# Two quads of value products per visit, maxima padded to 128 columns, and re-dealt places in a cross-attention and expert kernel

## The reference

```python
q = layernorm(x) @ Wq.T + bq;  k = ctx @ Wk.T + bk;  v = ctx @ Wv.T + bv
qk = einsum('bhqd,bhkd->bhqk', q, k)              # no scale
attn = softmax(qk);  z = einsum('bhqk,bhkd->bhqd', attn, v)
a = layernorm(z + layernorm(x)) * gamma + beta;   x2 = x + a
zf = layernorm(layernorm(x2)) * g + b             # then the router
w = top-2 of softmax(zf @ rW + rb), normalised over the two
out = x2 + sum_e w_e * (gelu(zf @ W1_e + b1_e) @ W2_e + b2_e)
```

## Time and profile before

| | |
|---|---|
| median of 3 runs | 846.84 us (845.5 to 849.79) |
| profiled execution, its own time | 850.93 us |
| its span, first to last instruction | 848.7 us |
| mean granted TensorE clock | 0.943 of 2.4 GHz |

### The profile page before, as it was taken

How to read it: one execution, slowest core, us unless ns; L and a number is a source line. 1 busy time by engine, 2 the same in 40 slices (tenths; PEclk the granted TensorE clock), 3 DMA queues, 4 the chain that set the end, 5 groups by cost and what they waited for, 6 DMA issues and landing times.

```text
span 848.7 us, 26242 instructions
## 1 busy us (share of the span) xinstructions
PE 755.9 (89%) x8056; PEld 586.7 (69%) x8057; DVE 631.7 (74%) x1779; ACT 563.4 (66%) x1469; POOL 535.6 (63%) x609
## 2 busy tenths in 40 slices
PE   3689999999999999999999997565979888999994
PEld 2456667767777777777777675344968787999994
DVE  7488998889899998998998898875446673454441
ACT  3346777888888887888888885533655544666662
POOL 3323667677677676876777775317456555777773
PEclk9989999999999999999999999855989998999998
DMA  6756575768768677677687676621334333443441
GB/s 186 170 122 144 125 159 123 161 148 179 161 150 189 140 172 165 152 170 169 147 183 160 160 169 147 195 59 43 57 55 63 51 46 56 75 63 57 67 62 21
DMA packets 154000, 104.43 MB, mean 123 GB/s; under 512 B 68364, under 2 KB 149560, under 8 KB 153816
## 3 DMA queue, kind: packets, MB, share of 16 engines
q1 hardware_dynamic: 133462, 77.42, 41.8%
q0 software_dynamic: 10944, 14.10, 10.3%
q10 hardware_dynamic: 9538, 12.23, 5.1%
HBM read 36.65 MB, written 17.33 MB: 64 GB/s over the span
## 4 chain that ended last, share of the span: by engine, by line
PE 62%; DMA 11%; DVE 8%; issue 6%; POOL 6%; SPq 4%; ACT 2%; DVEq 1%; ACTq 0%; POOLq 0%
PE s_row L988 9%; PE pj L884 8%; PE pj L853 8%; PE s_row L898 7%; PE s_t L917 7%; PE zt L929 7%; PE pj L999 4%; PE zt L999 4%; PE pj L871 3%; SPq L653 2%; DMA stack_x<-in_x 2%; DMA out_x<-index_space,idx_s 2%; DMA zscr<-zn 2%; DVE negmax L1360 2%; DMA stack_x<-k_part 2%
## 5 line engine op out<-in xcount | busy, mean ns | idle before, releaser
L1360 DVE TENSOR_REDUCE negmax<-s_row 100x1 f32<-100x361 f32 x512 | 251.5, 524 | 24.8 <-PE s_row L898 18.9
L1183 ACT ACTIVATE p_t<-s_t 128x400 f32<-128x400 f32 x384 | 187.9, 499 | 85.8 <-PE s_t L917 77.6
L898 PE MATMUL s_row<-stack_x,q_stack 125*128 125x361 bf16 x512 | 133.2, 322 | 18.7 <-DVE negmax L1360 12.8
L721 POOL DMA_INDIRECT out_x<-index_space,idx_s x57 | 92.2, 1617 | 76.3 <-ACT index_space L1168 34.6
L917 PE MATMUL s_t<-q_stack,stack_x 128*128 128x100 bf16 x1536 | 129.4, 211 | 10.9 <-ACT p_t L1183 8.7
L917 PEld LDWEIGHTS s_t<-q_stack,stack_x 128*128 128x128 bf16 x1536 | 93.5, 99 | 57.3 <-issue 30.9
L988 PE MATMUL s_row<-w_qkv,v_aug 128*128 128x128 f32 x912 | 117.8, 285 | 1.2 <-DVE v_aug L1455 1.2
L988 PEld LDWEIGHTS s_row<-w_qkv,v_aug 128*128 128x128 f32 x912 | 113.0, 202 | 1.8 <-DVE v_aug L1455 1.7
L1365 DVE TENSOR_SCALAR p_t<-p_t 128x1200 f32<-128x1200 f32 x128 | 100.0, 781 | 12.8 <-ACT p_t L1183 12.7
L884 PE MATMUL pj<-w_qkv,ct 128*128 128x256 f32 x384 | 106.0, 399 | 0.0
L853 PE MATMUL pj<-ct,w_qkv 128*128 128x361 f32 x256 | 96.1, 500 | 10.3 <-DMA bk_s<-in_bk 9.2
(11 more groups left out here) (232 smaller groups left out, 1423.8 us busy)
## 6 DMA issues: line engine op xcount, KB each, us to landing
stack_x<-k_part SPq DMA_DIRECT2D x192, 192.0 KB, 3.6
q_stack<-q_part SPq DMA_DIRECT2D x192, 64.0 KB, 2.0
ct<-in_ctx_t SPq DMA_DIRECT2D x32, 361.0 KB, 4.3
stack_x<-in_w ACTq DMA_DIRECT2D x8, 512.0 KB, 6.7
w_s<-in_w ACTq DMA_DIRECT2D x14, 256.0 KB, 2.9
zscr<-zn SPq DMA_DIRECT2D x32, 100.0 KB
z_in<-zscr SPq DMA_DIRECT2D x32, 100.0 KB
zf_d<-zf_s SPq DMA_DIRECT2D x32, 100.0 KB
```

The lines of the kernel that those rows point to most:

```text
L721: pool.indirect_dma_start(out_rows[0:n], bass.IndirectOffsetOnAxis(idx_s[:, k.slot:k.slot + 1], 0), ys[:, k.slot, :], None, bounds_check=n ...
L898: nc.tensor.matmul(s_row[h % 2][:, 0:KEYS], q_stack[0:MROW, b.slot, h, :], k_stack[0:MROW, b.slot, h, 0:KEYS], start=True, stop=True).then ...
L1183: nc.scalar.activation(p_t[:, quad % 2, kt, :], s_t[g % 2][:, 0:4 * Q], ACT.Exp).then_inc(exp_done, 1)
L1360: v.tensor_reduce(negmax[:, b.slot, h:h + 1], s_row[h % 2][0:Q, 0:KEYS], AXIS.X, ALU.max, negate=True).then_inc(max_done, 1)
```

## The change

Five things are changed.

1. `values` is called for two quads back to back, in slots 0 and 6 of an iteration, in place of one quad in slots 0, 3, 6 and 9. `p_t` gets a third quad, indexed by `ring`.
2. `m_rows` gets 128 columns, of which 80 are zero, and its transpose writes 128 partitions.
3. `v_raw` is gone to make room: the bias writes `v_aug` and the cleaning works in place. The routing words that used its space move to `k_rest`; `ys` of the expert part moves into `p_t`, and the first expert result waits for the last value products.
4. The places of the pipeline's steady part are changed.
5. The places of batch 0 (`START`) are changed.

```diff
+def ring(b, quad):
+    return (b.slot + quad) % 3
...
-        v_raw = sb(es, "v_raw", [128, KT * H, DH])
-        p_t = sb(es, "p_t", [128, 2, KT, 4 * Q])
+        p_t = sb(es, "p_t", [128, 3, KT, 4 * Q])
...
-            m_rows = sb(att, "m_rows", [Q, 3 * H], BF16)
+            m_rows = sb(att, "m_rows", [Q, 128], BF16)
...
-                    nc.tensor.matmul(tr[0:3 * H, 0:Q], m_rows[:], ident_bf[:], start=True, stop=True).then_inc(mt_done, 1)
+                    nc.tensor.matmul(tr[:, 0:Q], m_rows[:], ident_bf[:], start=True, stop=True).then_inc(mt_done, 1)
...
-                    pe.wait_ge(p_ready, G * b.index + quad + 1)
+                    if quad % 2 == 0:
+                        pe.wait_ge(p_ready, G * b.index + quad + 2)
...
-                                                    p_t[0:n, quad % 2, kt, j * Q:j * Q + Q], start=(kt == 0), stop=(kt == KT - 1))
+                                                    p_t[0:n, ring(b, quad), kt, j * Q:j * Q + Q], start=(kt == 0), stop=(kt == KT - 1))
...
-                        if n.valid() and g % KT == 0:
+                        if n.valid() and g in (KT, 3 * KT):
+                            values(n, g // KT - 1)
                             values(n, g // KT)
...
-                        after(act, pv_done, G * b.index + quad - 1)
-                    nc.scalar.activation(p_t[:, quad % 2, kt, :], s_t[g % 2][:, 0:4 * Q], ACT.Exp).then_inc(exp_done, 1)
+                        after(act, pv_done, G * b.index + quad - 2)
+                    nc.scalar.activation(p_t[:, ring(b, quad), kt, :], s_t[g % 2][:, 0:4 * Q], ACT.Exp).then_inc(exp_done, 1)
...
-                    v.scalar_tensor_tensor(v_aug[:, b.slot, :, 0:DH], v_raw[:], 0.0, v_raw[:], ALU.max, ALU.min).then_inc(v_ready, 1)
+                    biased = v_aug[:, b.slot, :, 0:DH]
+                    v.scalar_tensor_tensor(biased, biased, 0.0, biased, ALU.max, ALU.min).then_inc(v_ready, 1)
...
-SP_PLACE = {"zf": 7, "ctx": 3, "q": 14, "k": 14, "zout": 4, "max": 10, "zin": 14}
+SP_PLACE = {"zf": 1, "ctx": 6, "q": 12, "k": 17, "zout": 9, "max": 11, "zin": 12}
...
-START = {"PE": {"k0": 3, "k1": 3}, "ACT": {"k0": 0, "drow": 1, "k1": 1, "dt": 2, "q": 3, "k_mid": 3, "q_mid": 7}, "DVE": {}, "POOL": {"k_rest": 3, "k_low": 11}, "SP": {}}
+START = {"PE": {"k0": 5, "k1": 13}, "ACT": {"k0": 1, "drow": 0, "k1": 3, "dt": 0, "q": 3, "k_mid": 9, "q_mid": 13}, "DVE": {}, "POOL": {"k_rest": 11, "k_low": 17}, "SP": {}}
```

More of the change, by code:

```diff
@@ L479, in build @@
             q_stack = sb(att, "q_stack", [128, 3, H, QPAD], BF16)
-            index_space = sb(att, "index_space", [128, KT * D])
+            index_space = sb(att, "index_space", [128, 4 * NT])
             negmax = sb(att, "negmax", [Q, 3, H])
-            m_rows = sb(att, "m_rows", [Q, 3 * H], BF16)
+            m_rows = sb(att, "m_rows", [Q, 128], BF16)
             m_rest = sb(att, "m_rest", [Q, H])
@@ L541, in build @@
             base = per_expert(drow[:])
-            idx_at = index_space
-            ys, idx0, idx1, slot_c, second = carve(idx_at, (2 * D, NT, NT, NT, NT))
-            ys = ys.rearrange("p (s d) -> p s d", s=2)
+            idx0, idx1, slot_c, second = carve(index_space, (NT, NT, NT, NT))
+            ys = p_t[:].rearrange("p r k n -> p (r k n)")[:, 0:2 * D].rearrange("p (s d) -> p s d", s=2)
             idx_t = [idx0, idx1]
@@ L1287, in _ @@
                 v.memset(q_part[:, :, :, :, Q:QPAD].rearrange("p a s t k -> p (a s t) k"), 0.0).then_inc(pad_written, 1)
+                v.memset(m_rows[:, 3 * H:], 0.0).then_inc(pad_written, 1)
                 dve.wait_ge(rows_written, 2)
@@ L1338, in values_biased @@
                 def values_biased(b, last):
-                    after(dve, v_ready, b.index)
+                    after(dve, pv_done, G * (b.index - 2))
                     if last:
                         dve.wait_ge(v2_done, b.index + 1)
-                        v.tensor_tensor(v_raw[:, 2 * H:3 * H, :].rearrange("p h d -> p (h d)"), pj[0][:, 0:D],
-                                        bv_s[:, :], ALU.add).then_inc(v2_biased, 1)
+                        v.tensor_tensor(v_aug[:, b.slot, 2 * H:3 * H, 0:DH], pj[0][:, 0:D].rearrange("p (h d) -> p h d", d=DH),
+                                        bv_s[:, :].rearrange("p (h d) -> p h d", d=DH), ALU.add).then_inc(v2_biased, 1)
                     else:
                         dve.wait_ge(v01_done, b.index + 1)
-                        bias2 = bv_s[:, :].unsqueeze(1).broadcast_to([128, 2, D])
-                        v.tensor_tensor(v_raw[:, 0:2 * H, :].rearrange("p (t h) d -> p t (h d)", t=2), pj[1][:, :].rearrange("p (t n) -> p t n", t=2),
-                                        bias2, ALU.add).then_inc(v01_biased, 1)
+                        bias2 = bv_s[:, :].rearrange("p (h d) -> p h d", d=DH).unsqueeze(1).broadcast_to([128, 2, H, DH])
+                        v.tensor_tensor(v_aug[:, b.slot, 0:2 * H, 0:DH].rearrange("p (t h) d -> p t h d", t=2),
+                                        pj[1][:, :].rearrange("p (t h d) -> p t h d", t=2, d=DH), bias2, ALU.add).then_inc(v01_biased, 1)
                 def values_cleaned(b):
-                    after(dve, pv_done, G * (b.index - 2))
                     dve.wait_ge(v2_biased, b.index + 1)
                     dve.wait_ge(v01_biased, b.index + 1)
-                    v.scalar_tensor_tensor(v_aug[:, b.slot, :, 0:DH], v_raw[:], 0.0, v_raw[:], ALU.max, ALU.min).then_inc(v_ready, 1)
+                    biased = v_aug[:, b.slot, :, 0:DH]
+                    v.scalar_tensor_tensor(biased, biased, 0.0, biased, ALU.max, ALU.min).then_inc(v_ready, 1)
                 def row_max(b, h):
@@ L1364, in guard @@
                     dve.wait_ge(exp_done, NG * b.index + KT * quad + KT)
-                    v.tensor_scalar(p_t[:, quad % 2], p_t[:, quad % 2], 0.0, None, ALU.max).then_inc(p_ready, 1)
+                    v.tensor_scalar(p_t[:, ring(b, quad)], p_t[:, ring(b, quad)], 0.0, None, ALU.max).then_inc(p_ready, 1)
                 heads = tr[0:Q, :].rearrange("q (h w) -> q h w", w=32)
@@ L1462, in result @@
                     after(dve, scattered[k.slot], 16 * k.pair)
+                    if k.known and k.index == 0:
+                        dve.wait_ge(pv_done, G * B)
                     v.tensor_scalar(idx_s[:, k.slot:k.slot + 1], idx_t[1][:, bass.ds(k.index, 1)], 0.0, None, ALU.add).then_inc(idx_s_ready, 1)
```

11 lines of the change are left out of this document (6 added, 5 removed).

## The result

The changed kernel takes 858.64 us (857.64 to 860.58, 4 runs) where the kernel before takes 846.45 (845.5 to 849.79, 4 runs) beside it: ratio 1.0137, 95% interval 1.0113 to 1.0161. It is slower by 1.4%. The forecast was 846.5 us with the range 836 to 853; both missed. The profiled execution has a span of 858.8 us against 848.7.

The account below looks back on a forecast made before the run. SP's queue, 15.46 us per batch, was to take over from PE as the bound. 850.9 - 1.4 + 1.5 - 0.5 = 850.5 us; that difference, -0.4, put on the median 846.84 gave 846.5 us, range 836 to 853.

Parts of the forecast that it names:

- PE's gain, 0.68 us per batch: PE's stream per batch: paired visits save 0.48 us and padded maxima 0.205, leaving 14.85 us.
- The last step of the sum for the whole time: Whole kernel: the difference of -0.4 us put on the median of 846.84 was said to give 846.5 us.
- What else the edits cost: DVE, ACT and the memset: nothing taken, since DVE even at 14.6 us per batch stays under the period.
- waits for maxima: PE waiting for DVE's maxima in slots 7 and 8: period 15.1 to 15.5 us, with no chance of its own.
- SP's ring: SP's queue, once per batch through its own `zscr` store: 14.36 us plus 1.1 for moved stores, 15.46 us.
- the term "1.1" for the stores: SP's queue: stores of `zf` and `x` between queries and keys add 1.1 us per batch, bounds 0.8 and 3.4.
- The rival in which the stores hold up the keys: Key DMAs behind 200 KB of stores: the kernel loses once the ring grows over 0.07 us past 15.46; chance 0.2.
- my sign for stores that cost more than 1.1: Profile after, regular part: a period over 15.6 us would say that the stores cost more than 1.1 us.
- The first rival: Regular part: the `zscr` store lands sooner or stores need less, PE's pace is reached, 834 or 840 us; chance 0.25.
- The start: Batch 0: PE begins at about 12 us, not 9.21; 1.5 us lost, first transposed maxima at 51 to 53.
- nothing, if the load is hidden: Lower bound for batch 0's loss: no time lost if the load of `x` is hidden.
- The last batches: Last batches: PE's shorter stream saves at most three times 0.68 us; 0.5 us taken as gain.

Follow-up runs that it names:

- e5: The kernel before with only `m_rows` padded to 128 columns; ratio 0.9945 to the kernel before, turn 15.32 us.
- e10: e6 with quads 2 and 3 visited together in quad 3's slot; ratio 1.0126 to the kernel before, turn 15.82 us.
- e6: e1 with the products of one quad per visit again; ratio 0.9951 to the kernel before, turn 15.34 us.
- e3: The changed kernel with ACT copying the transposed maxima in slot 11, not 12; ratio 1.0127 to the kernel before, turn 16.07 us.
- e1: The changed kernel with all place tables and the start table of the kernel before; ratio 1.0046 to the kernel before, turn 15.68 us.
- e7: e1 with DVE's guard on the exponentials covering one of three key groups; one execution, 848.36 us, turn 15.58 us.
- e12: e6 with SP's stores of `zf` and `x` between the query and key DMAs; ratio 1.0026 to the kernel before, turn 15.63 us.
- e4: The changed kernel with `zf`'s transposes back in PE's slot 3 and ACT's slot 4, router in PE's slot 6; ratio 1.0074 to the kernel before.
- e13: The changed kernel with ACT issuing the expert weights' loads ahead of slot 1, behind the maxima's copy; ratio 1.0040 to the kernel before.
- e14: The kernel before with ACT copying the transposed maxima in slot 12; ratio 1.0001 to the kernel before, turn 15.53 us.

## Why the prediction was wrong

**PE's gain, 0.68 us per batch: right.** e5 measures the padding's part at 0.21 us, and in the changed kernel the double visit and the transpose have the starts that I worked out. (The last step of the sum for the whole time gives 846.4, not 846.5; nothing hangs on it.)

**"What else the edits cost": this step failed.** I held DVE's 14.1 us of work against the period and took nothing. An engine with free time can still be waited for at a certain place: a visit to `values` covered DVE's bias and two maxima between the projection of `v` and that of the keys. Pairing quads 2 and 3 takes that cover away and gains nothing, and the double visit is paid elsewhere (e10, +0.48 us per batch against e6). I had named waits for maxima among the rivals and waved them into the forecast.

**The tables: I followed SP's places and not the others'.** The three places listed ahead of the prediction leave out ACT's order and PE's slots for `zf` and the router; with the new numbers these moved too. The regular turn, 15.57 but for two late ones, has three rings within 0.1 us of one another: `zf` through POOL, ACT and PE's slots 2 and 4 (seen in the waits, shown by e3), the handing over between PE and DVE (e1, e7), and SP's ring (e12, and SP's waits in the changed kernel and e4). Taking away the first left the turn where it was (e4).

**SP's ring: the mechanism was right, the size off.** SP no longer waits for `k_low`, `zf` issues in 0.32 us; the term "1.1" for the stores is 1.2 and the sum 15.63 in place of 15.46, on the losing side of 15.53. The rival in which the stores hold up the keys named the point from which it decides, 0.07 us over my sum, and e12 lies past it; so does my sign for stores that cost more than 1.1, a period over 15.6. In the changed kernel SP's round has no slack in 17 of eighteen turns, and the two turns in which PE waits for the keys are 1.8 of the 2.5 us. The first rival had the store to `zscr` landing sooner once `zf` and `x` no longer follow it; it took 5.1 to 5.4 us as before.

**The start: 1.5 us were too many.** PE begins at 11.58, about as forecast, but the first maxima are at 49.6 and not at 51 to 53. The late load of `x` covers the delay: it is issued at 26.73 and takes 16.20 us, where it was 26.23 and 17.22. This is the case "nothing, if the load is hidden". That it is even earlier than before means little: in one execution each, the twelve kernels with the old start have their first maxima at 46.4 to 50.3 us, the six with the new one at 48.3 to 49.6.

**The last batches: the largest miss.** I took -0.5 us for them by scaling PE's saving. They have +4.8, and +3.1 follow, where I took nothing; up to the first expert product it is 8.7 together, 121.5 in place of 112.8 us from the 28th maxima on. The copy of the maxima moved by one slot, from the last of a turn to the first of the next, and past the weights' loads at that boundary. e13 puts it at 8 us of the 12 by the timed runs, with an uncertainty of 3; its trace shows 5.1 of the 8.7. What is left, 3.4 us by the ratio of e13, fits the regular part's 2.5.

Open: why e14's collision is free; what holds e4's turn; and how the last batches' loss splits. e1, in which the copy stands ahead of the loads, also takes 70.2 us for the last four batches, and has caught most of it up by the first expert product (114.1 us from the 28th maxima). The stretch behind the last maxima varies from 302.6 to 309.2 us over these kernels' single executions.

## What to carry to other kernels

Before moving work off an engine that is the bound, look at what that work was covering: find the two steps on either side of it and subtract their starts, with and without; a view of waits that leaves short pieces out shows nothing of it. When a table of places is dealt anew, follow every number that crosses a turn's boundary past what is issued once at that boundary (loads for the next stage above all), and every wait on an in-order queue that something urgent now stands behind. And when a large re-dealing comes with a good idea, time the idea alone first: the padding by itself was worth 0.55%, with one pairing 1.0%, and all of it together -1.4%.

## What the runs showed of the hardware

A bf16 transpose with 128 weight columns costs 0.2 us less from the product ahead of it to the one behind than one with 48 (e5, 15.53 to 15.32 us per batch).

The issue of the 100 KB store `zf`, 2.63 us right behind the `zscr` store, takes 0.32 to 0.37 behind the query transfers, and the stores then cost the queue 1.2 us, 0.5 more than their two issues (e12).

The maxima's transfer, 9.4 KB, took 6.75 us to land where the weights' loads (512 KB each) are issued ahead of it and 6.29 where they are issued right behind it (e13); at other times the chain of the kernel before has 3.23 and 4.00 us for it.
